# Router logits of two mixture-of-experts layers: narrow weights held still in four column groups, tokens moving, and one transpose back

## The reference

```python
logits = tokens.astype(jnp.float32) @ gate_weight.astype(jnp.float32).T   # [8192, 256] @ [256, 8]
probs = jax.nn.softmax(logits, axis=-1)
top1 = jnp.argmax(logits, axis=-1)
...
gates = jax.nn.softmax(xt @ wg, axis=-1)                                  # second mixture
expert_idx = jnp.argmax(gates, axis=-1)
```

## Time and profile before

| | |
|---|---|
| median of 3 runs | 1897.93 us |
| lowest, highest | 1897.42, 1899.61 us |
| span of the profiled execution, first to last instruction | 1900.1 us |
| the profiled execution's own time | not given apart from its span |
| mean granted TensorE clock | 0.986 of full speed |
| TensorE busy | 1843.4 us, 97% |
| VectorE busy | 1496.8 us, 79% |
| ScalarE busy | 1069.6 us, 56% |
| GpSimd busy | 624.2 us, 33% |
| share of TensorE in the chain that ended last | 86% |

### The profile page before, as it was taken

The page is one execution under the profiler, slowest core; times in us unless marked ns, Lnnn a source line. Parts: engine busy times, 40 slices in busy tenths (PEclk is TensorE's granted clock), DMA queues, the critical chain, the costliest instruction groups (busy, mean ns, idle before and its releaser), DMA issues.

```text
span 1900.1 us, 31592 instructions
## 1 busy us (share of the span) xinstructions
PE 1843.4 (97%) x11542; PEld 1631.5 (86%) x11542; DVE 1496.8 (79%) x3901; ACT 1069.6 (56%) x1734; POOL 624.2 (33%) x927
## 2 busy tenths in 40 slices
PE   8999999999999999999899999999999999999996
PEld 7888878888888888888779998888988799999996
DVE  7777579999999999999748884789998566666663
ACT  5656725566566665666456663665564255555552
POOL 3211001234433333444604443134534312333333
PEclk9999999999999999999899999999999899999998
DMA  5545242222222221201143422134322312222210
GB/s 178 163 150 167 81 153 68 90 86 95 89 84 83 94 82 64 78 26 37 51 152 124 134 87 89 60 119 135 100 89 76 90 60 82 93 83 86 76 51 18
DMA packets 132610, 176.95 MB, mean 93 GB/s; under 512 B 11486, under 2 KB 115813, under 8 KB 132328
## 3 DMA queue, kind: packets, MB, share of 16 engines
q1 hardware_dynamic: 121704, 159.87, 26.3%
q0 software_dynamic: 10752, 15.06, 2.3%
HBM read 113.25 MB, written 76.51 MB: 100 GB/s over the span
## 4 chain that ended last, share of the span: by engine, by line
PE 86%; DVE 5%; ACT 2%; POOL 2%; DMA 2%; issue 2%; SPq 0%; POOLq 0%; DVEq 0%; ACTq 0%
PE ps L385 78%; PE ps L409 4%; PE ps L712 2%; PE ps L701 1%; POOL d_p L2587 1%; DVE bst L1614 1%; PE ps L470 1%; DMA stage<-in_w 0%; DMA stage<-in_wi 0%; DVE rO L2155 0%; DMA xa<-in_x 0%; DVE wslotA L1820 0%; DMA d_x<-df 0%; DVE pay L1939 0%; DVE kl L1639 0%
## 5 line engine op out<-in xcount | busy, mean ns | idle before, releaser
L385 PE MATMUL ps<-wslotA,fh 128*128 128x256 f32 x1776 | 326.1, 284 | 0.0
L1830 DVE TENSOR_TENSOR fl<-fF,fh 128x512 fp32r<-128x512 f32 x316 | 214.0, 683 | 94.2 <-ACT fF L1209 93.3
L385 PEld LDWEIGHTS ps<-wslotA,fh 128*128 128x128 f32 x1776 | 280.4, 191 | 5.2 <-DVE fl L1830 0.2
L385 PE MATMUL ps<-wslotA,fl 128*128 128x256 f32 x888 | 251.2, 283 | 0.0
L2582 POOL TENSOR_TENSOR smalls<-smalls,powers 128x4 f32<-128x4 f32 x87 | 28.0, 321 | 591.7 <-DVE smalls L1617 591.6
L2587 POOL DMA_INDIRECT d_p<-pay,sut x128 | 154.3, 1205 | 103.7 <-DVE pay L1987 57.4
L385 PE MATMUL ps<-x2h,wslotA 128*128 128x512 f32 x512 | 171.0, 396 | 0.2 <-DVE x2l L1639 0.2
L385 PEld LDWEIGHTS ps<-wslotA,fl 128*128 128x128 f32 x888 | 170.0, 191 | 0.0
L1208 ACT ACTIVATE fh<-ps,b1e 128x512 fp32r<-128x512 f32 x126 | 86.9, 690 | 143.0 <-PE ps L385 140.6
L385 PE MATMUL ps<-wslotB,fh 128*128 128x256 f32 x752 | 137.1, 283 | 0.4 <-DVE fl L1830 0.4
L385 PE MATMUL ps<-eh,wslotB 128*128 128x512 f32 x384 | 125.3, 393 | 2.4 <-DVE el L2011 2.4
(11 more groups left out here) (383 smaller groups left out, 5146.5 us busy)
## 6 DMA issues: line engine op xcount, KB each, us to landing
stage<-in_w SPq DMA_DIRECT2D x16, 1024.0 KB, 5.6
d_p<-blank SPq DMA_DIRECT2D x24, 528.0 KB, 4.8
pay<-d_p SPq DMA_DIRECT2D x24, 528.0 KB, 3.7
d_x<-df SPq DMA_DIRECT2D x16, 516.0 KB, 3.5
xA<-d_x SPq DMA_DIRECT2D x16, 516.0 KB, 3.7
xa<-in_x SPq DMA_DIRECT2D x16, 512.0 KB, 4.9
d_h<-hh SPq DMA_DIRECT2D x16, 512.0 KB, 5.4
d_h<-hl SPq DMA_DIRECT2D x16, 512.0 KB, 3.0
```

Source lines behind the costliest of these rows:

```text
L385: return pe.matmul(o, a, b, start=start, stop=stop, skip_group_check=True)
L1830: ve.tensor_tensor(dl[:, half(k)], df_[:, half(k)], f32(dh[:, half(k)]), ALU.subtract).then_inc(S["low"], 1)
```

## The change

The logits are computed the other way round. `gwT` or `wgT`, 128 x 8, is the weight, 128 tokens move, and the four token tiles of a group write the partitions 0 to 7, 32 to 39, 64 to 71 and 96 to 103 of one unit (named LA): `ps[32 * i:32 * i + 8, 0:128]`. ScalarE copies the 128 x 128 result to a new SBUF tile `lgt` (`logits_copy`), and TensorE transposes it once into a unit LG (`by_token`), where `route1` reads the columns 32i to 32i+7. A step of the attention stage takes 16 units in place of 15, one of the linear-attention stage 20 in place of 18. VectorE's `route1` stands later in the attention stage (behind `new_x`) and, for the odd group, in the other one (behind `k_relu`); one `route_exp` of ScalarE moves one place. The load of `b1e` is counted on another semaphore.

```diff
+        lgt = sb("lgt", [128, 128])[:, :]
...
             def logits(which, g, x, w8):
                 evacuated("TT", which, g)
                 if g == 0:
                     evacuated("RW")
-                ps = unit("LG", which, g)
-                for i in range(4):
-                    for c in range(2):
-                        t = pe.matmul(ps[:, i * 8:i * 8 + 8], x[:, c * 512 + i * 128:c * 512 + i * 128 + 128], w8[:, c, :],
-                                      start=c == 0, stop=c == 1)
-                t.then_inc(S["lg"], 1)
+                ps = unit("LA", which, g)
+                for c in range(2):
+                    for i in range(4):
+                        t = mm(ps[32 * i:32 * i + 8, 0:128], w8[:, c, :], x[:, c * 512 + i * 128:c * 512 + i * 128 + 128],
+                               c == 0, c == 1)
+                t.then_inc(S["la"], 1)
+
+            def by_token(which, g):
+                evacuated("LA", which, g)
+                pe.transpose(unit("LG", which, g)[:, 0:128], lgt, ident).then_inc(S["lg"], 1)
...
                 if s + 2 in GROUPS:
                     attend(s + 2, 0)
                     attend(s + 2, 1)
+                if s - 2 in GROUPS:
+                    by_token(0, s - 2)
                 if s in GROUPS:
                     ff_in(s, 2, 0)
                     w2(s, 0)
...
             logits(0, 15, tT, gwT)
+            unread(a12_h, 2)
+            by_token(0, 15)
             unread(a12_h, 4)
             prefix(0, 15)
...
                 if s in PAIRS:
                     keys(2 * s + 1, 1)
+                if s - 2 in PAIRS:
+                    by_token(1, 2 * s - 3)
+                if s in PAIRS:
                     state(2 * s, 1)
                     queries(2 * s + 1)
...
                 if s in PAIRS:
                     state(2 * s + 1, 1)
+                if s - 1 in PAIRS:
+                    by_token(1, 2 * s - 2)
...
             logits(1, 15, tTO, wgT)
-            unread(wq_h, 4)
+            unread(wq_h, 2)
+            by_token(1, 15)
+            unread(wq_h, 2)
             prefix(1, 15)
...
+            def logits_copy(which, g):
+                u = ring.of("LA", which, g)
+                n = 16 * which + g
+                if n:
+                    act.wait_ge(S["lg"], n)
+                act.wait_ge(S["la"], n + 1)
+                copy(lgt, u.ap[:, 0:128]).then_inc(u.free, 1)
...
                 if s + 2 in GROUPS:
                     exponent(s + 2)
+                if s - 2 in GROUPS:
+                    logits_copy(0, s - 2)
                 if s - 1 in GROUPS:
                     norm_4th(s - 1)
                 if s + 1 in GROUPS:
...
                 if s + 1 in PAIRS:
                     xl_high(2 * s + 2)
+                if s - 2 in PAIRS:
+                    logits_copy(1, 2 * s - 3)
                 if s in PAIRS:
                     kv_high(2 * s + 1, 0)
...
-                ve.tensor_tensor(L, v3(u.ap[:, 0:32], 4, 8), r.unsqueeze(2).to_broadcast([128, 4, 8]),
+                ve.tensor_tensor(L, v3(u.ap[:, 0:128], 4, 32)[:, :, 0:8], r.unsqueeze(2).to_broadcast([128, 4, 8]),
                                  ALU.mult).then_inc(u.free, 1)
...
                 if s + 1 in GROUPS:
                     difference(s + 1)
-                if s - 2 in GROUPS:
-                    route1(0, s - 2)
                 if s + 1 in GROUPS:
                     weighed(s + 1)
                 if s + 2 in GROUPS:
                     attended(s + 2, 0)
                 if s - 1 in GROUPS:
                     new_x(0, s - 1)
+                if s - 2 in GROUPS:
+                    route1(0, s - 2)
...
-            load(b1e[:, :], io["eb1_c"], S["b1e"])
+            load(b1e[:, :], io["eb1_c"], S["late"])
```

More of the change, by code:

```diff
@@ L121, in build @@
             "nm_l", "xn_l", "xlT", "xlh", "q", "qh", "ql", "kv", "kf", "kvh", "kvl", "kva", "vw", "vwh",
-            "kwh", "kw", "ao", "nm_o", "xo", "b1e", "wout", "rs_o", "xr", "var_o")}
+            "kwh", "kw", "ao", "nm_o", "xo", "wout", "rs_o", "xr", "var_o")}
         free = [sem(f"free{i}") for i in range(3)]
@@ L922, in tensor_program @@
             w2(14, 2)
+            by_token(0, 12)
             x2_t(15)
@@ L940, in tensor_program @@
             t_t(0, 14)
+            by_token(0, 13)
             pe.wait_ge(S["o"], G)
@@ L944, in tensor_program @@
             prefix(0, 13)
+            by_token(0, 14)
             unread(a12_h, 20)
@@ L1029, in tensor_program @@
             logits(1, 13, tTO, wgT)
-            unread(wq_h, 12)
+            unread(wq_h, 2)
+            by_token(1, 13)
+            unread(wq_h, 10)
             t_t(1, 14)
@@ L1034, in tensor_program @@
             logits(1, 14, tTO, wgT)
-            unread(wq_h, 4)
+            unread(wq_h, 2)
+            by_token(1, 14)
+            unread(wq_h, 2)
             prefix(1, 14)
@@ L1487, in scalar_program @@
             hidden(14, 3, 1, ACT.Silu, b1_c)
+            logits_copy(0, 12)
             x2_high(15)
@@ L1500, in scalar_program @@
             t_turned(0, 13, tT)
+            logits_copy(0, 13)
             t_turned(0, 14, tT)
+            logits_copy(0, 14)
             route_exp(0, 13)
@@ L1504, in scalar_program @@
             t_turned(0, 15, tT)
+            logits_copy(0, 15)
             route_exp(0, 14)
@@ L1557, in scalar_program @@
                     v_copy(2 * s + 1, 1)
+                if s in PAIRS:
+                    kv_high(2 * s + 1, 1)
                 if s - 2 in PAIRS:
                     route_exp(1, 2 * s - 3)
-                if s in PAIRS:
-                    kv_high(2 * s + 1, 1)
                 if s - 1 in PAIRS:
@@ L1570, in scalar_program @@
                     v_copy(2 * s + 2, 0)
+                if s - 1 in PAIRS:
+                    logits_copy(1, 2 * s - 2)
                 if s in PAIRS:
@@ L1577, in scalar_program @@
                     route_exp(1, 2 * s - 2)
-            act.wait_ge(S["b1e"], 16)
+            act.wait_ge(S["late"], 96)
             for n in range(E - 1, 3 * E):
@@ L2489, in vector_program @@
                     lows(xAl[(2 * s + 2) % 2], xAh[(2 * s + 2) % 2], ring.of("XLT", 2 * s + 2), S["xlh"], 2 * s + 2)
-                if s - 2 in PAIRS:
-                    route1(1, 2 * s - 3)
                 if s in PAIRS:
@@ L2494, in vector_program @@
                     k_relu(2 * s + 1, 1)
+                if s - 2 in PAIRS:
+                    route1(1, 2 * s - 3)
                 if s - 1 in PAIRS:
```

## The result

The changed kernel takes 1915.4 us (median of 4 runs, 1913.4 to 1916.6), the kernel before 1897.7 beside it (4 runs): a ratio of 1.0091, 95% interval 1.0077 to 1.0106, 17.7 us slower. The prediction was 1908, range 1894 to 1931, slower with a chance of 0.75. Sign and range hold; of the 17.7 us it had 10, and they are not made up as it said.

The account below looks back on a forecast made before the run. TensorE, busy 97% of 1900.1 us, was taken as the bound. Terms of +14.6 us (attention-stage wait), -4.4 (linear-attention stage) and -0.4 (group 12, first router) gave +10 on 1897.9: 1908 us, range 1894 to 1931.

Parts of the forecast that it names:

- Removed, 1.78: TensorE, per group: 1.70 us of old logits records and 0.08 of lag in `attend` would go.
- Width changes, 0.29: TensorE, around the new logits: changing from 128 weight columns to narrow ones and back would add 0.29 us.
- Streaming, 0.98: TensorE, the 16 new logits records: products starting in order overlap only partly, taking 9 slots, 0.98 us.
- the bound: TensorE, the new logits: four column groups at once would stream in 0.44 us, saving 0.94 per group.
- Rival 2: Logits: four column groups at once, 1895 us, chance 0.15; second part, shorter ScalarE chain too, 1887 us, chance 0.08.
- The wait in the attention stage: Before `ff_in(s, 2, 0)`: TensorE waits for `attended` to free its PSUM unit; steps grow 1.22 us on average, +14.6 total.
- Moving `route1` ... out of the way doesn't help: VectorE, attention stage: moving `route1` (1.45 us) would not help, because `tanh` is now what is late.
- Rival 3: After attention-stage pauses: half clock for 3.4 us behind every other one, +10 us more, 1918 us; chance 0.07.
- The linear-attention stage, -4.4: No new wait there, VectorE's work staying under the 35.0 us step; about 11 groups save 0.40 each, -4.4 us.
- The ends of the routers, 0 with 1.5 either way: Last group's logits to `route1`: extra copy and transpose (0.8 us) against a shorter product (0.8 less); net 0, 1.5 either way.
- The second `attend` unit: Attention stage: emptied some 4.8 us after the first, while its next product comes 5.4 us later; close, but no wait.
- The semaphore of `b1e`: The load of `b1e`, counted on another semaphore: satisfied long before it is asked for, cost 0.

Follow-up runs that it names:

- r1: The changed kernel with the attention stage's transpose moved behind `ff_in(s, 2, 1)` and `route1` behind `low(s, 2, 0)`: 1889.4 us, 0.9955 of the kernel before.
- r7: r1 with the logits written tile by tile, both contraction halves of one tile before the next, instead of half by half: 1888.2 us.
- r2: The changed kernel with ScalarE's attention-stage copy of the logits put behind `tanh` instead of ahead of `norm_4th`: 1900.7 us.
- r3: The changed kernel with five products of 512 columns that nobody reads put ahead of `ff_in(s, 2, 0)` in the attention stage: 1907.7 us.
- r8: The changed kernel with the attention stage's `route1` put back ahead of `weighed` on VectorE, where it stood before: 1957.7 us.
- r4: The changed kernel with VectorE's `stats_o` moved ahead of `k_relu(2s+1, 0)` in the linear-attention stage: 1916.7 us.

## Why the prediction was right or wrong

- **Removed, 1.78: right.** 1.70 between the starts, and 0.08 behind: before, the second product of `attend` starts 0.30 after the first (453.55), where 0.22 is usual. That product in the kernel before, then in r1:

```profile
453.85 0.38 PE L385 MATMUL ps<-xl,sc 128*128 128x258 f32 x1
```

```profile
451.53 0.38 PE L386 MATMUL ps<-xl,sc 128*128 128x258 f32 x1
```

- **Width changes, 0.29: right.** In r1 it is 0.21 in place of 0.12 ahead of the first record, 0.20 in place of 0.11 behind the last, and 0.32 in place of 0.22 from the first `attend` product to the second (451.21, 451.53): 0.28 together. At that last place 0.08 goes and 0.10 comes, so `attend` lasts 3.65 us (451.21 to 454.86) where it lasted 3.63. The transpose starts 0.31 behind the last narrow product (457.46, 457.77), as `ff_in` did before, so that change is not paid twice.
- **Streaming, 0.98: mis-sized.** The step that failed is "If products start in order, only the second record of one tile can run beside the first of the next". Four groups run at once: the last of the 16 records starts 0.35 us after the first, with its own 0.11 that is 0.46, where the bound said 0.44; and r7 shows that their order does not even matter. Rival 2's first part is what happened, at 0.15. From the first record of the logits to the first of `ff_in` r1 needs 4.21 us, before it was 5.33; less 0.09 ahead of the logits and 0.11 for the transpose, the saving is 0.92 per group, where I had 0.40 and the bound said 0.94. By the Trainium skill (TensorE: Matmul & The Clock Gate, Part 3, Measured speedup vs the span model) tiles of the array start about 4 ns apart; the trace agrees in kind, four records start within 0.04 us. The Trainium skill (the same page, The mechanism) also says that matmuls start and end strictly in program order; r7's starts don't fit that, and as ends are modelled in the trace, no run here shows it for the ends.
- **The wait in the attention stage.** Place, chain and unit as forecast, each link 0.4 us earlier since the logits end earlier: copy at T + 0.84, `norm_4th` T + 1.01, `weighed` T + 4.13, `attended` done T + 6.35, `ff_in` at T + 6.41 (T is 453.48, the first record less the 0.09 of the width change). The growth without the clock is 9.5 / 11 = 0.86 per step; 1.22 was forecast, 0.68 with the true streaming (most of the difference lies ahead of the copy, which starts at T + 0.84 where rival 2 had the logits end at T + 0.69). r1, r2 and r3 show the cause; r8 shows that "Moving `route1` ... out of the way doesn't help" was wrong as written: where it stood, `route1` would wait for the transpose, so the move is worth more than 2 us per step, only it doesn't free the unit in time.
- **The clock.** Rival 3, at 0.07, came true beside the forecast: 7.7 us, not 10. It should have been a term of the sum and not a rival: I had the pause of 1.8 us and a row with a fall behind 2.2 us.
- **The linear-attention stage, -4.4: wrong.** For the ten groups of the five steps that is -4.0, and with the true saving -9.2; it was -2.0. The step that failed is "VectorE's work per step ... stays under the new 35.0". That is an average, and the average of VectorE did not change (32.98 against 33.00). What holds TensorE is the order: the transpose, `route1`, `stats_5th`, `kw_low`, `lows`, `keys`. I looked at the units of the new instructions alone and not at the unit behind them, whose owner waits in VectorE's queue behind `route1`, and `route1` now waits for something later than before: it starts 0.27 us after `xl_t` (1300.27, 1300.54), before it started 1.2 us ahead of it. So `keys` starts 1.40 us behind the products of `prefix` (1303.97 to 1305.37) where it was 0.10, which is 6.5 of the 7.2 us that are missing.
- **The ends of the routers, 0 with 1.5 either way: right.** The first one, TensorE before and then after, there with the last group's `route1` on VectorE:

```profile
918.79 1.85 PE L712 MATMUL ps<-gwT,tT 128*128 128x8 f32 x16
...
942.44 0.21 PE L385 MATMUL ps<-oht,tri 128*128 128x32 bf16 x1 [2.17 <-DVE oht L1967]
```

```profile
934.89 0.62 PE L386 MATMUL ps<-tT,gwT 128*8 128x128 f32 x16
...
957.75 0.19 PE L386 MATMUL ps<-oht,tri 128*128 128x32 bf16 x1 [2.06 <-DVE oht L2008]
...
956.15 0.19 DVE L1997 TENSOR_TENSOR lgx<-ps,pay 128x32 f32<-128x32 f32 x1
```

  From group 13's logits to group 15's `prefix` it is 23.65 us before and 22.86 after, though three products are each 1.15 us shorter. For the last group it is VectorE's queue that binds: its `route1` starts at 956.15, behind an op on the next weights (954.84 to 956.05), while the transpose is done at 954.8. In the second router it is 3.43 us from the last logits to `prefix` before (1490.93 to 1494.36) and 3.35 after (1504.40 to 1507.75).
- **The second `attend` unit** held: no other wait appeared in the stage. The semaphore of `b1e` cost nothing that the trace shows.

In sum, for the 11 attention steps 13.4 us were forecast and 9.5 came, the clock added 7.7 that the forecast left out, and the five linear-attention steps gave 2.0 in place of 4.0. The sign follows from the mechanism; that the size came out inside the range rests on a larger saving, an overlooked wait and an unpriced clock that happened to offset each other, and that part is luck.

## What to carry to other kernels

A faster product in a kernel whose buffers go round is worth its time only if the turn it adds to the ring does not land on a late buffer: list, for each take behind the new one, who frees the buffer and what that one stands behind in its queue. Here the same product costs 17.7 us in one order and gives 16 in another, with no instruction more or less. A stage's average load of the second engine does not tell this; the chain from the new instruction to the next wait of the bounding engine does. And a repeated pause of TensorE is to be priced with the clock that may fall behind it.

## What the runs showed of the hardware

- Four products in different column groups run at once, and by the times of r7 a group with work does not wait for the order of the program: 16 records of 128 columns go in 0.56 us in four groups and 1.85 in one, start to the next product's start.
- Plain fp32 does not stand in the way of that, although each product is two records.
- Of the twelve pauses in the changed kernel, five of the six of 1.72 to 1.79 us were followed by 3.4 us at 0.50 of the clock, none of the six of 1.35 (in r4, with the same pauses, four and none); in r2 none of twelve of 0.92, in r8 each of twelve of 3.83 (ten stretches of 6.8 us, two of 3.4). So the length of the pause alone does not decide it. A stretch of 3.4 us costs some 1.5 us, and five products of 0.23 us that nobody reads, put into the pause, took it away (r3).
